# Taking two exponentials ahead of a single PSUM copy on ScalarE, in a software-pipelined attention kernel

## The chip, the core and the metric

One NeuronCore of a Trainium2 chip runs the whole program. The metric is device time in microseconds of one execution; for the kernel before, the median of 3 runs is 1517.59 us (1516.69 to 1521.7).

## What is computed

Eight images of 32x32 tokens with 192 channels go through two blocks, each with a normalisation ahead and a residual behind. The first is attention over the 1024 tokens with 12 heads of 16 channels; the second is a Fourier mixer with a per-token linear layer beside it. Cut to what matters:

```python
x = x + attention(group_norm(x), w_qkv, w_o)      # softmax(q k^T / 4) v, 12 heads, 1024 tokens
x = x + fourier_mixer(group_norm(x), w1, b1, w2, b2, bias_w, bias_b)
# mixer: rfft2 over 32x32, two complex 48x48 block layers with relu, irfft2, + x @ bias_w.T + bias_b
```

## The kernel before, in words

The work is a pipeline over images, written out by hand and fully unrolled: `body(b, prep, post)` for b = 0 to 7, between a prologue and a tail, once for each engine. A body has 48 **steps** (`u`, three groups of four heads by 16 key/half tiles). In each step:

- TensorE makes four **score tiles** of 128 keys by 512 queries (L1215) into three PSUM banks `scores`, and the **value product** of the step before into `o_acc` (L1268).
- ScalarE takes the exponential of each score tile into `probs` (L931). At steps with s = 9 and s = 0 it also copies the attention output out of `o_acc` (`take_o`, L939).
- TensorE makes four **max tiles** for attention 11 steps ahead, q times k again with the queries on partitions (L1247), and VectorE reduces each to its row maximum (L1023). Max 1 to 4 below are these four of one step.
- SP issues every DMA, in an order fixed by the program.

Beside this run the **pieces**: the preparation of image b+1 (`prep`: transposes `turn`, statistics, q/k and v products) and the rest of image b-1 (`post`: output projection, transposes, spread of the normalisation's factors, Fourier transforms `dftw`, `dfth`, mixing `mix1`, `mix2`, the inverses, and `lin`, the linear layer). TensorE makes a piece into PSUM; ScalarE copies it out for turn, spread, v, dftw, dfth, mix1, mix2 and idfth, VectorE for the others (q/k takes both). Tables `PREP_AT` and `POST_AT` say at which step a piece runs and in which of two places: at the **head** of the step (START) or in its **middle** (MID). The kinds of `PAIRED` (qk, v, proj, lin) enter as two entries, each with a PSUM bank of its own.

The order on TensorE within a step is: head pieces, max 1, score 1, max 2, score 2, value product of the step before, middle pieces, score 3, max 3, score 4, max 4. Max and score tiles use different halves of the array's rows, and are issued as neighbours. On ScalarE it is: take_o at s = 9, head pieces, exponentials 1 and 2, take_o at s = 0, middle pieces, exponentials 3 and 4. A score tile waits for the exponential three tiles back (`probs_made`, three banks).

Pieces and max tiles share the PSUM tile `ring`, of four banks. `RING_ORDER` lists everything that goes into it in TensorE's order, entry n uses bank n % 4, and `bank_free` makes TensorE wait, ahead of entry n, until the engine that reads entry n-4 is done with it:

```python
    for u in range(IN_BODY):
        out += pieces_at(u, START) + [("max", u, 0), ("max", u, 1)]
        out += pieces_at(u, MID) + [("max", u, 2), ("max", u, 3)]
        ...
```

`jobs_of` gives ScalarE's and VectorE's list of pieces of a step's head or middle, each with its bank. The list holds an entry also for a piece that the other engine takes; the piece function then returns without an instruction.

What reads the copies next: SP regroups rows by DMA behind each dftw copy (`regroup_rows`, L671), behind dfth (`stack_spectrum`, L680), mix2 (`regroup_mixed`) and idfth (`regroup_lines`). The same queue issues the stacks of q and k (L616, L621) and the shift rows (L630) that the first score tile of every eighth step waits for. VectorE's statistics read the transposes, POOL's `normalise_tokens` the spread.

Of the kernel before, what the change touches and what calls it, by code (L numbers as in the profile page):

```python
# [46 lines left out]
START, MID = 0, 1  # L47
# [87 lines left out]
def made(order, kind, k):  # L135

    return order[kind, k | 1 if kind in PAIRED else k] + 1
# [8 lines left out]
def on_act(kind):  # L146

    return kind in ON_ACT
# [109 lines left out]
def build(nc, consts, x, w_qkv, w_o, w1, b1, w2, b2, bias_w, bias_b, out):  # L258
# [3 lines left out]
    with ctx:  # L262
# [134 lines left out]
        def after(eng, s, count):  # L397

            if not isinstance(count, int) or count > 0:
                eng.wait_ge(s, count)  # L400
# [16 lines left out]
        def batches(eng, prologue, body, tail):  # L417

            prologue()
            body(0, True, False)  # L420
            for b in range(1, NB - 1):
                body(b, True, True)
            body(NB - 1, False, True)
            tail()

        def spectrum_piece(k, bank_):

            chunk, kk = divmod(k, 3)
            if kk == 2:
                return spec[:, chunk, :, 448:NF], bank_[0:CH, 0:C].rearrange("p (r f) -> p r f", r=2)  # L430
            n = 4 - kk
            src = bank_[0:CH, 0:P * n].rearrange("p (j r f) -> p r j f", j=n, r=2)
            return spec[:, chunk, :, 256 * kk:256 * kk + 64 * n].rearrange(
                "p r (j f) -> p r j f", j=n), src

        def hidden_piece(k, bank_):
            blk, half = divmod(k, 2)
            return (hidden[0:CH, blk, NF // 2 * half:NF // 2 * (half + 1)], bank_[0:CH, 0:NF // 2],
                    mix_a_bias[:, blk:blk + 1])
# [7 lines left out]
        def early_bank(no):  # L447
            return scores[:, no % EARLY_BANKS, :]

        def late_bank(kind, k):  # L450
            return late_banks[POST_NO[kind, k] % LATE_BANKS]

        def ring_bank(entry):
            return ring[:, RING_NO[entry] % RING, :]
# [26 lines left out]
        def pieces_of(b, u, part, prep, post):  # L481

            late = post and not (isinstance(b, int) and b < 2)
            return [e for e in pieces_at(u, part)
                    if (prep if e[0] == "prep" else late if e[1] == 2 else post)]

        def jobs_of(b, u, part, prep, post, prep_piece, post_piece):

            return [(prep_piece if e[0] == "prep" else post_piece, b - e[1], *e[2:], ring_bank(e))
                    for e in pieces_of(b, u, part, prep, post)]  # L490
# [6 lines left out]
        def late_pieces(post_piece):  # L497

            for n, (kind, k) in enumerate(in_order(LATE)):
                post_piece(NB - 2, kind, k, ring[:, n % RING, :])  # L500
# [22 lines left out]
        def token_tile(k):  # L523

            return k // 2 + NT // 2 * (k % 2)

        def token_quarter(k):

            at = HALF * (k % 2) + QUARTER * (k // 2 % 2)
            return slice(at, at + QUARTER)  # L530
# [392 lines left out]
        @block.scalar  # L923
        def _(act):
            def exponentials(b, g, s, h):
                n = g * TILES + s * GH + h
                act.wait_ge(scores_made, NG * TILES * b + n + 1)
                if h == 0:

                    after(act, pv_made, STEPS * NG * b + STEPS * g + s - 1)  # L930
                nc.scalar.activation(probs[:, GH * (s % 2) + h, :], scores[:, n % SCORE_BANKS, :], ACT.Exp,  # L931
                                     scale=SCALE).then_inc(probs_made, 1)

            def take_o(slot, half):
                act.wait_ge(pv_made, STEPS * slot + 8 * half + 8)
                if half == 0:

                    after(act, o_normed, slot)
                nc.scalar.copy(o_raw[:, HALF * half:HALF * (half + 1)],  # L939
                               o_acc[:, 0, :]).then_inc(o_out, 1)  # L940

            def prep_piece(b, kind, k, bank_):
                if kind != "qk" and not on_act(kind):
                    return
                act.wait_ge(prep_made, N_PREP * b + made(PREP_NO, kind, k))
                if kind == "turn":
                    nc.scalar.copy(xt[:, k, :], bank_).then_inc(prep_by_act, 1)
                if kind == "v":

                    after(act, v_ready, NG * b)  # L950
                    nc.scalar.copy(v_new[:, token_tile(k), :], bank_[:, 0:C]).then_inc(prep_by_act, 1)  # L951
                if kind == "qk":

                    for g in range(2 if k < 4 else NG):
                        after(act, stacked[g], STACK_INCS * b)
                        after(act, stacked_second[g], SECOND_INCS * b)
                    nc.scalar.copy(qk_parts[:, 0, k // 4, token_quarter(k)],  # L957
                                   bank_[:, 0:QUARTER]).then_inc(part0_done, 1)

            def post_piece(b, kind, k, bank_):  # L960
                if not on_act(kind):
                    return
                act.wait_ge(post_made, N_POST * b + made(POST_NO, kind, k))
                two = bank_[:, 0:2 * C].rearrange("p (t n) -> p t n", t=2)
                done = post_by_act
                if kind == "turn":
                    nc.scalar.copy(xt1[:, k, :], bank_).then_inc(done, 1)  # L967
                if kind == "spread":
                    nc.scalar.copy(affine[:, :, :], two).then_inc(done, 1)
                if kind in ("dftw", "idfth"):  # L970
                    nc.scalar.copy(rows_a[:, 2 * k:2 * k + 2, :], two).then_inc(done, 1)  # L971
                if kind == "mix2":
                    n = P if k < 4 else SIDE
                    nc.scalar.copy(mixed[0:n, k, :], bank_[0:n, 0:2 * C]).then_inc(done, 1)
                if kind == "dfth":
                    nc.scalar.copy(*spectrum_piece(k, bank_)).then_inc(done, 1)
                if kind == "mix1":
                    to, src, bias = hidden_piece(k, bank_)
                    nc.scalar.activation(to, src, ACT.Relu, bias=bias).then_inc(done, 1)  # L979

            def prologue():

                for no, (kind, k) in enumerate(PREP):
                    prep_piece(0, kind, k, early_bank(no))

            def body(b, prep, post):
                first = isinstance(b, int) and b == 0
                for u in range(IN_BODY):
                    g, s = divmod(u, STEPS)
                    slot = NG * b + g  # L990
                    if s == 9:
                        take_o(slot, 0)
                    for piece, *job in jobs_of(b, u, START, prep, post, prep_piece, post_piece):
                        piece(*job)
                    exponentials(b, g, s, 0)
                    exponentials(b, g, s, 1)
                    if s == 0 and not (first and g == 0):
                        take_o(slot - 1, 1)
                    for piece, *job in jobs_of(b, u, MID, prep, post, prep_piece, post_piece):
                        piece(*job)  # L1000
                    exponentials(b, g, s, 2)
                    exponentials(b, g, s, 3)

            def tail():
                take_o(NG * NB - 1, 1)
                late_pieces(post_piece)
                for kind, k in POST:
                    post_piece(NB - 1, kind, k, late_bank(kind, k))

            batches(act, prologue, body, tail)  # L1010


# [574 lines left out]
```

## Time and profile before

| | |
|---|---|
| median of 3 runs | 1517.59 us |
| the profiled execution | 1528.75 us |
| its span | 1527.0 us |
| granted TensorE clock, mean | 0.96 of full |
| TensorE, VectorE, ScalarE busy | 1445.3, 1158.3, 1009.0 us |
| 1536 exponentials | 829.0 us |
| 1536 maxima | 975.2 us |

The profiled execution is one run of the program and 11.16 us longer than the median. In the timelines, neighbouring instructions of one line and engine are merged into one row: its duration is from the first start to the last end, and x4 says how many there are. PEld is the loading of TensorE's weights, PE the matmul itself. A note in brackets is the idle time of that engine ahead of the row, and what ended it.

### The profile page before, as it was taken

What the parts mean: (1) busy time and instruction counts of PE and PEld (TensorE: products, weight loads), DVE (VectorE), ACT (ScalarE), POOL (GpSimd) and SP (SyncE); (2) the same over time, 40 slices, a digit from 0 to 9 for tenths busy, and PEclk for the clock granted to TensorE, in tenths of its full rate; (3) what the DMA queues carried; (4) which work ended last, traced back from release to release, by engine and by line L of the source; (5) the groups of instructions that cost most, each with busy time, mean ns of one, the idle gap of its engine ahead of it and who ended that gap; (6) DMA issues with size and microseconds to landing.
All of it is one profiled execution on the core that took longest, in us unless ns stands there. A gap on an engine that the chain in (4) does not pass through costs nothing.

```text
span 1527.0 us, 27399 instructions
## 1 busy us (share of the span) xinstructions
PE 1445.3 (95%) x9972; PEld 695.3 (46%) x9972; DVE 1158.3 (76%) x2153; ACT 1009.0 (66%) x2017; POOL 187.6 (12%) x277
## 2 busy tenths in 40 slices
PE   7699989999999999999999999999999999999787
PEld 4344333444545454444545444544544443434354
DVE  3695888888789878987789878997799878874131
ACT  1064777577767777677767777677767777668312
POOL 2000000140001300140011300040012100030000
PEclk7696999999999999999999999999999999999988
DMA  4430312213332414323422324333431333211313
GB/s 113 73 64 2 84 29 61 62 56 81 80 92 64 87 45 103 78 68 76 92 85 58 82 69 85 71 83 65 89 85 43 78 91 77 66 35 50 77 28 80
DMA packets 101126, 107.19 MB, mean 70 GB/s; under 512 B 25152, under 2 KB 77824, under 8 KB 100992
## 3 DMA queue, kind: packets, MB, share of 16 engines
q1 hardware_dynamic: 100992, 105.44, 30.1%
q8 instruction: 80, 1.31, 0.4%
q14 instruction: 54, 0.44, 0.1%
HBM read 27.51 MB, written 6.68 MB: 22 GB/s over the span
## 4 chain that ended last, share of the span: by engine, by line
PE 80%; DVE 6%; DMA 6%; SPq 2%; issue 2%; POOL 1%; ACT 1%; DVEq 0%; POOLq 0%; ACTq 0%
PE o_acc L1268 22%; PE ring L1247 15%; PE scores L1215 15%; PE ring L1291 10%; DVE row_max L1023 5%; DMA inv_all<-inv_rows 4%; PE ring L1280 3%; PE ring L1400 2%; PE ring L1393 2%; PE ring L1387 2%; SPq L663 2%; PE ring L1379 2%; PE scores L1291 1%; PE ring L1302 1%; PE ring L1406 1%
## 5 line engine op out<-in xcount | busy, mean ns | idle before, releaser
L1023 DVE TENSOR_REDUCE row_max<-ring 128x1 f32<-128x512 f32 x1536 | 975.2, 683 | 185.6 <-PE ring L1247 179.0
L931 ACT ACTIVATE probs<-scores 128x512 f32<-128x512 f32 x1536 | 829.0, 600 | 281.3 <-PE scores L1215 280.3
L1247 PE MATMUL ring<-k_stack,q_stack 48*128 48x512 f32 x1536 | 594.6, 469 | 26.7 <-DVE row_max L1023 24.3
L1215 PE MATMUL scores<-q_stack,k_stack 50*128 50x512 f32 x1536 | 598.7, 465 | 1.3 <-ACT probs L931 1.2
L1268 PE MATMUL o_acc<-probs,v_aug 128*18 128x512 f32 x3072 | 412.1, 609 | 2.4 <-ACT probs L931 1.2
L1215 PEld LDWEIGHTS scores<-q_stack,k_stack 50*128 50x128 f32 x1536 | 246.9, 188 | 319.6 <-ACT probs L931 294.9
L1247 PEld LDWEIGHTS ring<-k_stack,q_stack 48*128 48x128 f32 x1536 | 249.3, 191 | 145.4 <-DVE row_max L1023 97.3
L572 POOL TENSOR_TENSOR inv_all<-o_raw,inv_all 128x1024 f32<-128x1024 f32 x23 | 54.5, 2371 | 594.3 <-DMA inv_all<-inv_rows 594.3
L1268 PEld LDWEIGHTS o_acc<-probs,v_aug 128*18 128x18 f32 x3072 | 52.2, 96 | 124.5 <-issue 88.3
L1291 PE MATMUL ring<-xt,w_qk 64*128 64x256 f32 x504 | 62.3, 379 | 0.0
L1291 PE MATMUL ring<-wo,o_t 64*128 64x192 f32 x366 | 39.5, 346 | 16.1 <-DMA o_t<-inv_all 16.1
L1291 PEld LDWEIGHTS ring<-xt,w_qk 64*128 64x128 f32 x504 | 48.8, 186 | 9.1 <-DVE row_max L1023 3.9
L1095 DVE TENSOR_TENSOR x<-ring,x 128x192 f32<-128x192 f32 x60 | 18.8, 352 | 36.5 <-PE ring L1291 36.5
L1076 DVE TENSOR_TENSOR qk_parts<-ring,qk_parts 128x256 fp32r<-128x256 f32 x84 | 31.6, 417 | 18.9 <-ACT qk_parts L957 18.7
L1291 PEld LDWEIGHTS ring<-wo,o_t 64*128 64x128 f32 x366 | 34.2, 199 | 22.1 <-DMA o_t<-inv_all 10.5
L871 POOL COPY v_aug<-v_new 128x512 f32<-128x512 f32 x24 | 14.3, 620 | 241.8 <-ACT v_new L951 212.2
L957 ACT CAST qk_parts<-ring 128x256 fp32r<-128x256 f32 x84 | 27.2, 375 | 22.7 <-PE ring L1291 22.7
L826 POOL TENSOR_TENSOR calc<-mean_var,calc 128x3 f32<-128x3 f32 x16 | 3.1, 194 | 316.2 <-DVE calc L1098 232.4
L971 ACT COPY rows_a<-ring 128x384 f32<-128x384 f32 x59 | 28.5, 483 | 19.4 <-PE ring L1406 9.3
L967 ACT COPY xt<-ring 128x512 f32<-128x512 f32 x22 | 12.9, 586 | 37.8 <-PE ring L1280 37.8
L1400 PE MATMUL ring<-mix_b,spec_a 97*128 97x96 f32 (+1 forms) x304 | 37.2, 274 | 0.7 <-ACT spec_a L979 0.7
L1400 PEld LDWEIGHTS ring<-mix_b,spec_a 97*128 97x128 f32 (+1 forms) x304 | 33.2, 176 | 8.4 <-issue 7.3
(152 smaller groups left out, 1112.6 us busy)
## 6 DMA issues: line engine op xcount, KB each, us to landing
q_stack<-qk_parts SPq DMA_DIRECT2D x288, 64.0 KB, 2.2
k_stack<-qk_parts SPq DMA_DIRECT2D x144, 128.0 KB, 4.3
inv_all<-inv_rows SPq DMA_DIRECT2D x24, 512.0 KB
rows_b<-rows_a SPq DMA_DIRECT2D x128, 96.0 KB, 2.8
spec_b<-spec_a SPq DMA_DIRECT2D x64, 102.0 KB, 2.3
x_in<-in_x_dram SPq DMA_DIRECT2D x8, 768.0 KB, 5.0
x_res<-in_x_dram SPq DMA_DIRECT2D x8, 768.0 KB, 4.7
o_t<-inv_all SPq DMA_DIRECT2D x192, 32.0 KB, 1.9
```

Of the source, the lines that this page charges most:

```text
L572: ops.tensor_tensor(inv_all[:, :], o_raw[:, :], inv_all[:, :], ALU.mult).then_inc(o_normed, 1)
L663: sp.dma_start(o_t[to:to + HD, g, :], inv_all[32 * h:32 * h + HD, HALF * half:HALF * (half + 1)]).then_inc(o_packed, 16)
L931: nc.scalar.activation(probs[:, GH * (s % 2) + h, :], scores[:, n % SCORE_BANKS, :], ACT.Exp, scale=SCALE).then_inc(probs_made, 1)
L1023: nc.vector.tensor_reduce(row_max[:, which, m:m + 1], max_bank(g, unit, i), AX.X, ALU.max).then_inc(max_taken, 1)
L1076: nc.vector.tensor_tensor(qk_parts[:, 1, k // 4, cols], bank_[:, 0:QUARTER], qk_parts[:, 0, k // 4, cols].bitcast(F32), ALU.subtract).then ...
L1215: mm(scores[:, n % SCORE_BANKS, :], k_stack[rows, 2 * g + hp, P * kt:P * (kt + 1)], q_stack[rows, g, half, hp, :], start=True, stop=True). ...
L1247: mm(max_bank(g, unit, i), q_stack[rows, g, half, hp, P * qt:P * (qt + 1)], k_stack[rows, 2 * g + hp, HALF * which:HALF * (which + 1)], st ...
L1268: last = mm(o_acc[32 * h:32 * h + VW, 0, :], v_aug[:, g, kt, h, :], probs[:, GH * (s % 2) + h, :], start=(kt == 0), stop=(kt == NT - 1), s ...
L1280: last = mm(bank_[ROWS * half:ROWS * (half + 1), P * t:P * (t + 1)], src[:, t + NT // 2 * half, third::THIRDS], ident, start=True, stop=True)
L1291: out.append(mm(banks[half][:, 0:n], lhs, rhs, start=(c == 0), stop=(c == 2)))
L1379: last = mm(bank_[:, 0:2 * C], const("fw"), tok_n[:, 2 * k:2 * k + 2, :], start=True, stop=True)
L1400: last = mm(to[:, :, blk, :], hidden[:, blk, P * k:P * k + n], mix_b[:, blk, :], start=True, stop=True)
```

## The change

Where the head list of a step has at most one entry, ScalarE now runs the step's exponentials 1 and 2 first and the head's piece after them. Steps with two or more head entries keep their order, and so do all other engines. No instruction is added or removed.

```diff
-                    for piece, *job in jobs_of(b, u, START, prep, post, prep_piece, post_piece):
+                    heads = jobs_of(b, u, START, prep, post, prep_piece, post_piece)
+                    few = len(heads) <= 1
+                    for piece, *job in [] if few else heads:
                         piece(*job)
                     exponentials(b, g, s, 0)
                     exponentials(b, g, s, 1)
+                    for piece, *job in heads if few else []:
+                        piece(*job)
                     if s == 0 and not (first and g == 0):
                         take_o(slot - 1, 1)
                     for piece, *job in jobs_of(b, u, MID, prep, post, prep_piece, post_piece):
```

## Rows read from the trace of the kernel before

**Rows 1.** The page, part 1: busy time, share of the span, instructions.

```profile
PE 1445.3 (95%) x9972; PEld 695.3 (46%) x9972; DVE 1158.3 (76%) x2153; ACT 1009.0 (66%) x2017; POOL 187.6 (12%) x277
```

**Rows 2.** Windows, body 3: length, busy PE, PEld, DVE, ACT, POOL; clock, DMA, GB/s.

```profile
591.20:759.90 168.70, 168.02 (x1234) 81.00 (x1232) 142.52 (x268) 125.64 (x252) 24.25 (x32) 1.00 0.34 78
```

**Rows 3.** Timeline, step 15 of body 3: start us, us, engine, line, instruction.

```profile
642.17 0.50 PE L1215 MATMUL scores<-q_stack,k_stack 50*128 50x512 f32 x1
...
642.29 0.59 ACT L967 COPY xt<-ring 128x512 f32<-128x512 f32 x1 [0.22 <-PE ring L1280]
...
642.77 1.09 ACT L931 ACTIVATE probs<-scores 128x512 f32<-128x512 f32 x2
...
643.28 2.47 DVE L1023 TENSOR_REDUCE row_max<-ring 128x1 f32<-128x512 f32 x4
...
643.83 0.29 PEld L1247 LDWEIGHTS ring<-k_stack,q_stack 48*128 48x128 f32 x2
643.83 0.72 PE L1247 MATMUL ring<-k_stack,q_stack 48*128 48x512 f32 x2
...
644.36 1.08 ACT L931 ACTIVATE probs<-scores 128x512 f32<-128x512 f32 x2 [0.50 <-PE scores L1215]
...
644.49 1.13 PE L1280 MATMUL ring<-cst,x 128*64 128x128 f32 x16
```

**Rows 4.** Timeline, step 25 of body 3.

```profile
674.91 1.08 ACT L931 ACTIVATE probs<-scores 128x512 f32<-128x512 f32 x2 [0.59 <-PE scores L1215]
...
675.88 0.59 ACT L939 COPY o_raw<-o_acc 128x512 f32<-128x512 f32 x1
...
676.35 0.51 ACT L971 COPY rows_a<-ring 128x384 f32<-128x384 f32 x1
...
677.61 0.73 PE L1247 MATMUL ring<-k_stack,q_stack 48*128 48x512 f32 x2
```

**Rows 5.** Groups by form, ScalarE: xcount | busy us, mean ns of one | idle before.

```profile
L971 ACT COPY rows_a<-ring 128x384 f32<-128x384 f32 x59 | 28.5, 483 | 19.4 <-PE ring L1406 9.3 <-PE ring L1379 8.0 <-PE ring L1412 2.0
...
L967 ACT COPY xt<-ring 128x512 f32<-128x512 f32 x22 | 12.9, 586 | 37.8 <-PE ring L1280 37.8
```

**Rows 6.** Timeline, step 2 of body 3, behind the piece of step 1.

```profile
597.42 0.68 DVE L1023 TENSOR_REDUCE row_max<-ring 128x1 f32<-128x512 f32 x1
...
597.64 0.52 PE L1247 MATMUL ring<-k_stack,q_stack 48*128 48x512 f32 x1
...
598.15 0.18 PEld L1247 LDWEIGHTS ring<-k_stack,q_stack 48*128 48x128 f32 x1 [0.34 <-DVE row_max L1023]
598.15 0.49 PE L1247 MATMUL ring<-k_stack,q_stack 48*128 48x512 f32 x1
```

**Rows 7.** Timeline, TensorE weight loads of the second q/k pair, behind step 16.

```profile
649.17 0.55 PEld L1291 LDWEIGHTS ring<-xt,w_qk 64*128 64x128 f32 x6 [0.35 <-DVE row_max L1023]
```

**Rows 8.** Timeline, step 43 of body 3, weight load of its score 2.

```profile
742.03 0.18 PEld L1215 LDWEIGHTS scores<-q_stack,k_stack 50*128 50x128 f32 x1 [0.42 <-ACT probs L931]
```

**Rows 9.** Timeline, step 37 of body 3, weight loads of the v pair.

```profile
719.75 0.95 PEld L1291 LDWEIGHTS ring<-wv,xt 64*128 64x128 f32 x12 [0.85 <-DVE row_max L1023]
```

**Rows 10.** Timeline, SP and weight loads, bodies 3 and 1.

```profile
676.88 2.08 SPq L671 DMA_DIRECT2D rows_b<-rows_a  x2
...
688.55 2.52 SPq L671 DMA_DIRECT2D rows_b<-rows_a  x4
...
695.42 2.74 SPq L630 DMA_DIRECT2D q_stack<-shift  x4
...
694.25 0.46 PEld L1387 LDWEIGHTS ring<-cst,rows_b 128*96 128x96 f32 x4 [0.85 <-DVE row_max L1023]
...
700.41 0.19 PEld L1215 LDWEIGHTS scores<-q_stack,k_stack 50*128 50x128 f32 x1
...
270.78 1.31 SPq L630 DMA_DIRECT2D q_stack<-shift  x2
...
273.99 0.19 PEld L1215 LDWEIGHTS scores<-q_stack,k_stack 50*128 50x128 f32 x2 [0.23 <-DMA q_stack<-shift]
```

## The prediction

> **What bounds the kernel now.** I read the page first. TensorE is busy for 95% of the span, VectorE 76%, ScalarE 66% [rows 1]. Cut by image, body 3 gives TensorE 168.0 us of 168.7 at full clock, with VectorE at 142.5 and ScalarE at 125.6 [rows 2]. So a delay of TensorE is a delay of the kernel unless another chain covers it, and ScalarE has 43 us of idle time an image that costs nothing. Whether ScalarE does a copy before or after two exponentials matters only through what waits for it. That is read from single steps; I call a time z+0.57 when it lies 0.57 us behind the start of the step's first score matmul.
>
> The PSUM ring has four banks and is handed out in program order: head piece, max 1, max 2, max 3, max 4. The head piece and **max 4** of the same step therefore share a bank, and TensorE cannot start max 4 before ScalarE has copied the piece out. In step 15 of body 3 (z = 642.17) [rows 3] the copy runs from 642.29 to 642.88, the two exponentials from 642.77 to 643.86, and the weights of max 3 and max 4 load at 643.83 and 643.94 (two loads, together 0.29 us, of 0.18 each). Max 4 ends at 644.55, and the next piece starts at 644.49. The copy is over 1.06 us before its bank is wanted: today's slack.
>
> **What the change does, priced.** It removes and adds no instruction. It moves one ScalarE copy behind two exponentials in the steps whose head list has one entry: for a full image 0, 1, 4 (next image's transposes), 14, 15, 16 (transposes), 22, 25, 26, 28, 31, 34, 35, 37, 42, 46. The projections, "lin" and the q/k and v products enter as pairs, so their steps stay; steps 5, 7, 9 and 18 hold a single piece that VectorE takes, with nothing to move on ScalarE.
>
> *The new place of the copy.* Score 1 ends at z+0.50, and an exponential starts as little as 0.03 behind its score (third: 644.36, score over at 644.33); I take z+0.57, today's 642.77 being z+0.60. Back to back, ScalarE starts one operation every 0.48 to 0.49 us (1.08 for two, of 0.60 each), also from exponential to copy: 675.39, 675.88, 676.35 [rows 4]. So: exponentials at z+0.57 and z+1.06, copy at z+1.54. With the durations of [rows 5] it ends at z+2.13 (transposes, 0.59) or z+2.02 (the kinds of 0.48: 26, 28, 34, 35, 37, 42, 46). Step 31's copy is half as wide. The third exponential, at z+2.19, is not touched.
>
> *The price at max 4.* A released load starts 0.05 behind its releaser: maximum over at 598.10, load at 598.15; and its matmul ends 0.49 behind that [rows 6]. So max 4's weights load at z+2.18 instead of z+1.77, and it ends at z+2.68 instead of z+2.38: **+0.30 us**. The 0.48 copies: load z+2.07, end z+2.56, **+0.18**. Step 31, with its shorter copy, comes within hundredths of the present load: 0. Copies lying ahead of take_o in steps 0 and 16 push it and the third exponential by 0.2, which nothing waits for.
>
> *Which steps pass it on.*
> - 0, 4, 14, 15 go into a single piece and from there along TensorE. VectorE takes max 4, the last of four maxima in 2.47 us from 643.28 [rows 3], at 645.07 = z+2.90, and a max 4 ending at z+2.68 is still in time. Full: 4 x 0.30 = 1.20.
> - 1 goes into a "lin" pair. The following step's second matmuls wait for VectorE's maximum (load 598.15, 0.34 idle); that maximum follows from max 3, which is not delayed. The first pair starts at 597.94 instead of 597.64, the second would end at 598.70 (first's end 598.46 plus the 0.24 between ends in [rows 3]) against 598.64: **+0.06**. By the same cover 28, 35, 46 (0.18) cost 0.
> - 16 goes into two q/k pairs; the second waits 0.35 for VectorE [rows 7], which covers 0.30: 0.
> - 42: the next step's score 2 waits 0.42 for step 42's third exponential, which is not late [rows 8]: 0.18 is covered: 0.
> - 22: its second matmuls are late already, held by VectorE's maximum as in [rows 6], so max 4 is too; what is left of 0.18 is under 0.05: 0.
> - 25: take_o stands first; z = 675.89, exponentials 676.43 and 676.92, copy 677.41 to 677.91, load 677.96, end 678.45 against 678.34 [rows 4]: +0.10. It passes.
> - 26 and 34: followed by a q/k pair whose second matmuls run on TensorE's own pace, and by a single piece: 0.18 each.
> - 37 is different: its ring goes piece, max 1, max 2, v pair, so the bank is wanted in mid-step. The v weights load at 719.75 = z+1.65 [rows 9]; the copy would end at z+2.02, the load start at z+2.07: **+0.42**, and v copies, maxima and five mix1 pieces follow in line. Full.
>
> *The queues.* SP's DMAs for step 25 start 0.02 behind the dftw copy (676.88), and SP then issues almost without a break until 698.2 [rows 10]. The copy ends 1.05 later, so this train comes up to 1.05 later. Its last row transfer (the fourth of 2.52 us from 688.55, so issued at 690.4, with 2.5 to landing as below) is wanted by dfth, whose weights load at 694.25; the shift rows (the fourth of 2.74 us, issued at 697.5) are wanted by step 32's first score, whose weights load at 700.41. In body 1 that wait shows: last issue at about 271.45, the score held 0.23 until 273.99, so landing takes about 2.5. That leaves 1.3 and 0.4, plus the 0.28 by which TensorE is late itself, against at most 1.05. Between 0 and 0.37; SP's own pauses take some of it, and I take 0.15. The other moved copies meet an SP queue that is busy (26, 28, 46) or slack of over 0.4 (31, 42). POOL's use of the spread copy stands behind its own multiply of the attention output.
>
> **Sum.** An image in bodies 2 to 6: 1.20 + 0.06 + 0.10 + 0.36 + 0.42 + 0.15 = 2.29; five are 11.45. Body 1 has no late piece of an older image behind step 4, and the bare step after it is covered as behind 42: 1.99. Body 0 has only steps 0, 1, 4: 0.36. Body 7 has no q/k, v or transposes of a next image: 14, 15, 25, 34 = 0.88. Together 14.7 us. The profiled execution took 1528.75 (span 1527.0), 11 above the median of 1517.59; the added waits do not depend on that, so against its own time I expect 1543 profiled and 1532.3 as a median. A measurement of this kernel tells about 0.3% (4.6 us) from no change.
>
> **The load and a rule.** In [rows 3] max 4's load stands 0.11 behind max 3's, and in [rows 6] a held matmul starts with its load: load and matmul are held together, and the 0.11 of the load is paid. The Trainium skill (TensorE: Matmul & The Clock Gate, The mechanism) says that TensorE pulls weight loads ahead of matmuls in flight when they go to other rows. By that rule the weights would lie ready, and only the matmul would be late; by it the sum would be 8.8 in place of 14.7. The trace disagrees wherever a bank is the thing waited for: the load waits too.
>
> **Rivals.**
> - *Loads run ahead*, with only the matmul held: max 4 starts at z+2.18 against z+1.99, +0.19 for a transpose (four pass), +0.08 for the others (two pass), 25 nothing, 37 +0.31, SP 0.15: 1.38 an image in five bodies, less in the other three, 8.8 in all: 1526.4. For it: loads do lie ahead within a step. Against: [rows 6]. 0.13.
> - *Nothing is absorbed*: six transposes 1.80, 25 0.10, six others 1.08, 37 0.42, SP 0.25 = 3.65 an image, about 24.7 in all: 1542. For it: VectorE is close behind, and the covers are as narrow as 0.05. Against: the idle times in [rows 7, 8]. 0.12.
> - *Hidden*: the copies come in time because max 4 is not what TensorE waits for, or the loss is taken up by VectorE's queue two steps on. 1518, at most 1522. Against: TensorE has 0.7 us of idle time in an image [rows 2]. 0.07.
> - *Faster*: the first two exponentials no longer stand behind a copy: 0.03 each in most steps (z+0.57 for z+0.60) and up to 0.3 in 22 and 25, where copy or take_o stood ahead; at most 1 an image, some 5 in all: 1512.5. It decides if a score or a value product waits for them. Score 4 needs the first one at z+1.77, and it is over at z+1.20 today; the value product waits for the fourth. 0.05.
>
> My forecast has 0.63. The range 1523 to 1541 takes in the lower price and most of the unabsorbed case. Faster 0.05, same 0.07, slower 0.88.
>
> **What the profile after would show.** Max 4's load with an idle time ended by the ScalarE copy (xt, rows_a or spec_a), some 0.4 us in steps 0, 4, 14, 15, and those steps 0.30 longer; step 1 nearly unchanged, 42 unchanged; step 37 longer by 0.42; ScalarE's busy time the same. If steps 14 and 15 keep their length, the bank rule is read wrongly; if steps 28, 35, 42 grow by 0.18, the covers are.

## The result, and the profile after

The changed kernel takes **1545.8 us** (median of 4 runs, 1537.42 to 1550.97), the kernel before, on the same chip, 1519.64 (4 runs, 1516.69 to 1523.37): a ratio of 1.0166 [1.0112, 1.0219]. It is slower by 26 us; the forecast was slower by 14.7, 1532.3 us with a range of 1523 to 1541. Run again on another chip: 1544.06 us beside 1522.15, 1.0155 [1.0131, 1.0178]. The direction was right, the size too small, and the result lies outside the range.

The page of the changed kernel (busy us, share of the span, instructions) answers to [rows 1]:

```profile
span 1534.6 us, 27399 instructions
PE 1447.3 (94%) x9972; PEld 706.2 (46%) x9972; DVE 1162.4 (76%) x2153; ACT 1009.6 (66%) x2017; POOL 187.4 (12%) x277
```

Same instructions, same busy times. Lines from about 1000 on stand four higher than before: L1219 are the scores, L1251 the max tiles, L1284 the transposes, L1295 the other products, L1410 (before L1406) the first inverse Fourier stage, idfth; L1027 is the maximum. The windows of bodies 2, 3 and 4 (first score to first score; the columns of [rows 2]):

```profile
413.90:587.00 173.10, 170.06 (x1234) 83.61 (x1232) 143.22 (x268) 125.78 (x252) 24.24 (x32) 1.00 0.32 76
587.00:760.90 173.90, 171.42 (x1234) 84.13 (x1232) 143.06 (x268) 125.62 (x252) 24.22 (x32) 0.99 0.33 75
760.90:933.60 172.70, 170.22 (x1232) 83.67 (x1230) 143.17 (x268) 125.74 (x252) 24.22 (x32) 1.00 0.33 76
```

Body 3 took 168.70 before and grew by 5.2, of which 2.8 are no effect of the change: a longer wait for the attention output (1.84 us, before 0.43) and a stretch at half the clock behind it. The other two grew by 3.24 and 3.01.

**The hold.** The timeline of step 15 of body 3 in the changed kernel, whose z is 641.78 (start, duration, engine, line, instruction; in brackets the idle time and what ended it):

```profile
641.78 0.73 PE L1219 MATMUL scores<-q_stack,k_stack 50*128 50x512 f32 x2
...
642.35 1.08 ACT L931 ACTIVATE probs<-scores 128x512 f32<-128x512 f32 x2 [0.95 <-PE scores L1219]
...
643.32 0.59 ACT L967 COPY xt<-ring 128x512 f32<-128x512 f32 x1
...
643.96 0.18 PEld L1251 LDWEIGHTS ring<-k_stack,q_stack 48*128 48x128 f32 x1 [0.23 <-ACT xt L967]
643.96 0.50 PE L1251 MATMUL ring<-k_stack,q_stack 48*128 48x512 f32 x1
...
644.39 0.36 PEld L1284 LDWEIGHTS ring<-cst,x 128*64 128x64 f32 x6 [0.25 <-issue]
```

Against [rows 3]: the copy runs at z+1.54 to z+2.13, max 4's weights load 0.05 behind its end at z+2.18, and not 0.11 behind those of max 3; the matmul is over at z+2.68, and the next piece starts at z+2.61. The step is 0.29 us longer than before. What ended the idle time ahead of all 1536 max tiles (us, times):

```profile
  DVE row_max L1027: 112.6, 239
  issue: 26.9, 52
  ACT xt L947: 5.9, 22
  ACT xt L967: 4.9, 21
  ACT spec_a L979: 2.3, 6
```

In the kernel before this list has the spec_a line, the same to the tenth, and neither of the xt lines: the copies of 43 transposes now hold a max tile, for 0.25 us each. The idle times behind the shorter copies (0.13 in steps 26 and 34) stand in it under none of these names.

**Step by step.** I took the length of each step (first score to first score) in both traces. The growth is the same to 0.02 in bodies 2 to 6 where a step's lateness comes from the bank (but for step 25 of body 2, 0.19, and step 47 of body 6), and scattered where it comes from a DMA:

| steps | forecast, us | measured, bodies 2 to 6 |
|---|---|---|
| 0, 4, 14, 15 | 0.30 each | 0.29 each |
| 1 with 2 | +0.06 | +0.30 -0.24 |
| 16 | 0 | +0.08 |
| 22 | 0 | 0 |
| 25 | +0.10 | +0.12 |
| 26, 34 | 0.18 each | 0.18 and 0.17 |
| 28 with 29, 35 with 36, 46 with 47 | 0 | +0.19 -0.19 |
| 42 with 43 | 0 | +0.16 -0.16 |
| 37 | +0.42 | +0.48 |
| 31 with 32 (shift rows) | in the 0.15 for SP | +0.03, +0.04, +0.36, +0.24, +0.13 |
| 44 (idfth) | 0 | +1.24, 0, 0, 0, +0.49; body 7: +1.53 |

The bank part comes to 2.25 an image, 11.3 in five, 1.9 in body 1 (step 4's 0.30 comes back in step 5), 0.3 in body 0 and 1.15 in body 7: **14.6 us**, 13.8 forecast. Behind steps 31 and 44 come 0.8 and 3.3: **4.1 us**, 0.9 forecast. That makes 18.7.

**Where the 4.1 come from.** SP's timeline behind step 42 of body 7, six row transfers for idfth, first before, then after; their start is the end of ScalarE's copy at the head of step 42:

```profile
1409.94 1.35 SPq L689 DMA_DIRECT2D rows_b<-spec_b  x2
...
1413.31 0.62 SPq L692 DMA_DIRECT2D rows_b<-spec_b  x1
```

```profile
1416.85 1.35 SPq L689 DMA_DIRECT2D rows_b<-spec_b  x2
...
1420.23 0.62 SPq L692 DMA_DIRECT2D rows_b<-spec_b  x1
```

TensorE's timeline behind them, before and after:

```profile
1415.92 0.50 PE L1215 MATMUL scores<-q_stack,k_stack 50*128 50x512 f32 x2
1416.35 0.91 PE L1406 MATMUL ring<-rows_b,cst 128*128 128x384 f32 x2
```

```profile
1421.62 0.50 PE L1219 MATMUL scores<-q_stack,k_stack 50*128 50x512 f32 x2
1423.61 0.56 PE L1410 MATMUL ring<-rows_b,cst 128*128 128x384 f32 x1 [1.49 <-DMA rows_b<-spec_b]
```

Before, idfth starts 3.04 us behind the last issue (1416.35 against 1413.31). After, without its wait of 1.49, it would have started 1.89 behind it, so the train has lost 1.15 us against TensorE. The last transfer also landed 3.25 us behind its issue, in before 2.46. Before had 0.46 to spare: 1.15 + 0.79 - 0.46 = 1.48. Body 2 waits 1.20 (landing 4.08, before 2.73), body 6 waits 0.47 (3.35, before 2.49); in bodies 1 and 3 to 5 landing takes 2.46 to 2.88 and idfth doesn't wait.

*Why the last transfer lands late.* It is a small one, and in body 2 of the changed kernel the DMA view of its time in flight (570.42 to 574.50) shows, beside the data queue, a packet of the queue that the profile calls instruction:

```profile
q1 hardware_dynamic: 708, 0.60, 59.4%
q8 instruction: 1, 0.02, 1.3%
...
rows_b<-spec_b SPq DMA_DIRECT2D x1, 24.0 KB, 4.1
```

The 14 traces hold 112 of these trains. In 29 of them the last transfer takes over 2.6 us (2.64 to 4.08), and in every one of the 29 such a packet starts 1.24 to 1.93 behind its issue. In 81 of the other 83 none starts within the first 2.0 us, and these take 2.44 to 2.51; the last two have one at 1.76 and 1.90 and take 2.56 and 2.46. The packets come at the same places of the program, in bodies 2, 3, 6 and 7. Before, they start 1.93, 2.35 and 2.36 behind the issue in bodies 2, 3 and 6, and in body 7 after the landing; with the train later by 1.4 they start at 1.27, 1.66, 1.65 and 1.68. No run moved these packets by themselves, so that they cause the late landing is inferred from where they coincide. Without the late landings bodies 2 and 6 would not have waited, and body 7 only 0.7: some 2.5 of the 3.3 are owed to them.

**What of the difference is not the change.** The profiled execution of after took 1537.42 us, only 8.7 more than before's 1528.75. A good part of the gap to 18.7 is TensorE's clock: before's execution has a stretch at half the clock (granted 0.50, that is 1.2 GHz) in body 7 which after's has not. First before, then after at about the same time:

```profile
1329.60:1343.30 13.70, 13.70 (x55) 5.92 (x55) 8.53 (x16) 6.75 (x13) 5.47 (x9) 0.50 0.29 97
```

```profile
1330.00:1343.70 13.70, 12.99 (x83) 5.57 (x80) 11.69 (x24) 9.71 (x20) 2.32 (x10) 1.00 0.24 69
```

Steps 19 to 22 of that body took 5.0 us longer in before for it. Before was also slower in the prologue by 3.8 us (mean granted clock 0.72, after 0.81) and in body 0 by 4.2 (0.91, after 0.94). Bodies 1 to 6, at a mean of 1.00 in both, took 1016.1 in before and 1033.9 in after: 17.8 us for them alone, 15.7 of it in the table and most of the rest in body 3.

One execution of the kernel of experiment 3 took 1903 us, at a clock of 0.642, and is left out of every mean here. Over the 186 other executions of all kernels, each beside its mean granted clock, the time falls by 0.94 us for every 0.001 of clock within one kernel, and what is left over scatters by 1.9 us. I use that below: "at equal clock" is a difference of means taken to one clock, 0.970, with the half-width of its 95% interval in brackets. Its base is all 73 executions of before, on three chips, 1520.4 us. By chip they stand at 1519.7 (experiments 1 to 4), 1521.6 (5 to 8) and 1520.3 (9 to 12), so the chip alone can shift a figure by about 1. For the change it is **21.8 us** (1.3) and, again, 20.7 (2.5), in the middle 21.3; against before on its own chip alone the second is 19.4 (2.7). So of the 26 us, some 2.6 go with the clock: the ten executions of after had a mean of 0.967, those of before 0.970.

### The profile page after: what moved, and what is told of

Same layout as the page of the kernel before. It is cut to its first block, busy times and chain, and to the rows that moved or that the text cites. A ratio compares the mean times of both kernels' runs of the same rounds, so it can differ in the third digit from the quotient of the medians.

```text
span 1534.6 us, 27399 instructions
## 1 busy us (share of the span) xinstructions
PE 1447.3 (94%) x9972; PEld 706.2 (46%) x9972; DVE 1162.4 (76%) x2153; ACT 1009.6 (66%) x2017; POOL 187.4 (12%) x277
## 4 chain that ended last, share of the span: by engine, by line
PE 78%; DVE 7%; DMA 6%; SPq 3%; issue 2%; ACT 1%; POOL 1%; DVEq 0%; POOLq 0%; ACTq 0%
PE o_acc L1272 21%; PE scores L1219 16%; PE ring L1251 14%; PE ring L1295 9%; DVE row_max L1027 6%; DMA inv_all<-inv_rows 4%; PE ring L1284 3%; PE ring L1404 2%; PE ring L1391 2%; PE ring L1397 2%; SPq L663 2%; PE ring L1383 2%; PE scores L1295 1%; PE ring L1306 1%; PE ring L1410 1%
## 5 line engine op out<-in xcount | busy, mean ns | idle before, releaser
L1027 DVE TENSOR_REDUCE row_max<-ring 128x1 f32<-128x512 f32 x1536 | 976.0, 683 | 192.1 <-PE ring L1251 183.3
L1251 PE MATMUL ring<-k_stack,q_stack 48*128 48x512 f32 x1536 | 609.1, 471 | 25.9 <-DVE row_max L1027 22.8
L1219 PE MATMUL scores<-q_stack,k_stack 50*128 50x512 f32 x1536 | 590.5, 462 | 1.4 <-ACT probs L931 1.3
L1219 PEld LDWEIGHTS scores<-q_stack,k_stack 50*128 50x128 f32 x1536 | 244.2, 186 | 316.8 <-ACT probs L931 297.5
L1251 PEld LDWEIGHTS ring<-k_stack,q_stack 48*128 48x128 f32 x1536 | 252.9, 189 | 154.1 <-DVE row_max L1027 89.7
L1295 PE MATMUL ring<-xt,w_qk 64*128 64x256 f32 x504 | 63.4, 380 | 0.0
L1295 PE MATMUL ring<-wo,o_t 64*128 64x192 f32 x366 | 39.2, 344 | 16.7 <-DMA o_t<-inv_all 16.7
L1295 PEld LDWEIGHTS ring<-xt,w_qk 64*128 64x128 f32 x504 | 51.5, 186 | 3.7 <-DVE row_max L1027 1.6
L1080 DVE TENSOR_TENSOR qk_parts<-ring,qk_parts 128x256 fp32r<-128x256 f32 x84 | 31.9, 420 | 19.2 <-ACT qk_parts L957 18.9
L1295 PEld LDWEIGHTS ring<-wo,o_t 64*128 64x128 f32 x366 | 34.0, 197 | 22.4 <-DMA o_t<-inv_all 10.4
L971 ACT COPY rows_a<-ring 128x384 f32<-128x384 f32 x59 | 28.5, 483 | 20.5 <-PE ring L1410 12.5
L1295 PE MATMUL ring<-bias_t,xt 64*128 64x192 f32 x360 | 40.7, 336 | 0.0
```

The lines of the kernel that those rows point to most:

```text
L1027: nc.vector.tensor_reduce(row_max[:, which, m:m + 1], max_bank(g, unit, i), AX.X, ALU.max).then_inc(max_taken, 1)
L1080: nc.vector.tensor_tensor(qk_parts[:, 1, k // 4, cols], bank_[:, 0:QUARTER], qk_parts[:, 0, k // 4, cols].bitcast(F32), ALU.subtract).then ...
L1219: mm(scores[:, n % SCORE_BANKS, :], k_stack[rows, 2 * g + hp, P * kt:P * (kt + 1)], q_stack[rows, g, half, hp, :], start=True, stop=True). ...
L1251: mm(max_bank(g, unit, i), q_stack[rows, g, half, hp, P * qt:P * (qt + 1)], k_stack[rows, 2 * g + hp, HALF * which:HALF * (which + 1)], st ...
L1295: out.append(mm(banks[half][:, 0:n], lhs, rhs, start=(c == 0), stop=(c == 2)))
```

## The experiments

The theories. *Bank and queue*: the time is the bank held by the late copy (14.6), plus DMAs that start later (4). *Clock*: more idle time makes the clock fall, which costs the rest. *Covered chain*: before waits in bodies 1 to 5 for the rows of the attention output, o_t (the projections at step 10, 0.4 to 2.6 us in its trace); later steps ahead of it would be hidden there. Most experiments are one line: the set of steps in which the change acts. Each text of expectation was written before its run.

**1. The piece between the two exponentials.**

```diff
                     exponentials(b, g, s, 0)
-                    exponentials(b, g, s, 1)
                     for piece, *job in heads if few else []:
                         piece(*job)
+                    exponentials(b, g, s, 1)
```

> A single head piece is copied between exponentials 1 and 2 of its step, not behind both. Bank theory (the loss is max 4 and the v pair held for the piece's bank): the copy starts at z+1.06 and ends at z+1.65, so its bank is free at z+1.70, ahead of max 4's weight load at z+1.77; nothing is held, except some 0.05 us at step 37's v pair. Within 2 us of the kernel before, about 1518 us. Queue theory (the loss is in DMAs that start later behind the copies of steps 25 and 42): these copies are still 0.5 us later than before, so about half of the unexplained 10 us stays, 1523 us. Clock theory (any idle TensorE time costs extra by a lower granted clock): no idle time is added, so as before.

Measured: 1520.9 us beside 1519.65, 1.0019 [0.9996, 1.0042]; at equal clock +1.7 (1.2). The copy is over 0.5 earlier, before the bank is wanted. The list ahead of the max tiles:

```profile
  DVE row_max L1027: 124.4, 264
  issue: 27.0, 52
  ACT spec_a L979: 2.3, 6
  DVE tok_n L1106: 1.1, 6
  DVE qk_parts L1080: 0.3, 1
  DVE shift L1043: 0.2, 1
  ACT xt L947: 0.2, 1
```

The holds are gone, and with them about nine tenths of the cost. What is left shows in waits of 0.54 and 0.72 for idfth's rows, and in steps 31 with 32 longer by 0.23 and 0.10, 1.6 together: the queue part, at a lateness of 0.5. (The queue theory had expected half of 10 us.)

**2 to 4. The steps in three sets.** Covered: 1, 16, 22, 28, 31, 35, 46. Copies with DMAs behind them: 25, 42. Passing it on: 0, 4, 14, 15, 26, 34, 37. Together these are all 16. Edit (and the same with the other sets):

```diff
-                    few = len(heads) <= 1
+                    few = len(heads) <= 1 and u in (1, 16, 22, 28, 31, 35, 46)
```

> The change in steps 1, 16, 22, 28, 31, 35 and 46 alone, whose delay the next step was read to cover. Bank theory with covers: max 4 ends 0.18 to 0.30 us later in each of them, and the following step is shorter by as much; 0.08 an image is left behind step 16 and 0.05 behind step 1, together 1 us, 1519 us. Without covers: 0.30 x 2 + 0.18 x 3 = 1.14 us an image, 8 in all, 1526 us. Clock theory: the idle time of TensorE ahead of max 4 is there whether it is covered or not; if that idle time lowers the clock, this kernel is 4 us or more slower than before though its steps add nothing.

> The change in steps 25 and 42 alone, whose copies SP waits for. Bank theory: step 25 longer by 0.12 us in seven images, step 42 covered by step 43: 1 us. Queue theory: in addition TensorE waits for DMAs that start 1.05 and 1.45 us later, at the first idfth piece behind step 44 (up to 1.5 us in some images, 3 in all) and at the score of step 32 (0.1 to 0.35 us in four images): 4 to 5 us over the kernel before, 1522 to 1523 us. If the whole of the unexplained part sits here it is 10 us, 1529.

> The change in steps 0, 4, 14, 15, 26, 34 and 37 alone, whose delay was read to pass on. Bank theory: 4 x 0.29 + 0.18 + 0.18 + 0.48 = 2.0 us an image in five bodies, 1.7 in body 1, 0.3 in body 0, 0.9 in body 7: 13 us, 1531 us. Queue theory adds nothing here, no copy of a DMA train but that of step 26 is moved. Clock theory: the added idle time lowers the granted clock, and the whole of the missing 10 us comes on top: 1540 us. Chain theory: step 0's take_o stands behind the late copy, so the attention output of the last group reaches the projection at step 10 about 0.3 to 0.6 us later than TensorE itself is delayed, 0 to 0.3 us more in an image.

| set | time, before | ratio | at equal clock |
|---|---|---|---|
| covered | 1524.99, 1519.65 | 1.0030 [1.0011, 1.0050] | +3.2 (1.3) |
| 25, 42 | 1526.2, 1519.65 | 1.0032 [1.0016, 1.0049] | +5.9 (1.1) |
| passing | 1532.85, 1519.65 | 1.0079 [1.0059, 1.01] | +12.4 (1.1) |

The sums: 21.5 for the three, 21.3 for the whole. The effects add up within the scatter. Against before on their own chip the three are 3.9, 6.6 and 13.1, 23.6 together.

In the traces every step of a set behaves as in the whole change. *Covered*: 1 with 2 +0.05, 16 +0.08, the other pairs cancel, 0.13 an image; that is 0.8 in all, and the clock-corrected time says 2 to 3 more, for which I found no wait. By its median this set is 5.3 above before, at a mean clock of 0.968 against 0.970: that is what the clock theory had expected of it (4 or more), and between the two bank forecasts for it, 1519 and 1526 us, the time alone does not decide. The steps of the trace do: the covers hold. *25, 42*: 25 +0.12; behind 44 TensorE waits 1.06, 0.48 and 1.20; 31 with 32 grows by 0.24, 0.07, 0.20, 0.16 in four bodies, and step 30 by 0.33 and 0.10 in two: 4.7 of 5.9. *Passing*: 0.29 in 0, 4, 14, 15, 0.18 in 26, 0.17 in 34, 0.48 in 37, all bodies alike, steps 31 and 44 unchanged. It has most of the holds that lengthen a step, and a mean clock of 0.9698, that of before, and 1532.85 where the clock theory had expected 1540: against that theory.

**5. The change again,** as the anchor of another chip.

> The changed kernel once more, for its time and its granted clock over more executions. Bank theory and the queue's part together, as the parts run singly add up (+13, +4, +6 us): 1541 to 1543 us at the clock that the kernel before has, +22 us. If the added idle time of TensorE also lowers the clock (0.967 against 0.970 so far), the clock stays under that of the kernel before by 0.002 or more, and the difference is 25 us; by chance theory, the two clocks come out equal and the difference is 22.

The numbers stand above: 1.0155 [1.0131, 1.0178], 21.9 us. The mean clock was 0.9670 beside 0.9696, lower by more than the 0.002 that the clock theory had named, while the difference was that of the chance theory, 22 and not 25. This run does not decide between them.

**6 and 7. The steps in two sets, by what reads the copy.** No DMA reads the copy: 0, 1, 4, 14, 15, 16, 22, 34, 35, 37. Queue: 25, 26, 28, 31, 42, 46.

> The change in the ten steps whose copies no DMA reads: 0, 1, 4, 14, 15, 16, 22, 34, 35, 37. Bank theory: 4 x 0.29 + 0.05 + 0.08 + 0.18 + 0.48 = 1.95 us an image in five bodies, 1.7, 0.3 and 0.8 in the others, 12.5 us, 1532 us. If queue theory holds that is all that these steps cost, and the whole of the remaining 10 us is in the other six. If the extra is instead something that every moved copy brings, this one measures 16 us or more.

> The change in the six steps whose copies feed DMAs of SP: 25, 26, 28, 31, 42, 46. Bank theory: 0.12 + 0.18 us an image, 28, 31, 42 and 46 covered: 2.1 us, 1522 us. Queue theory: the DMAs of steps 25 to 31 and of step 42 start later, TensorE waits for them behind step 44 and at step 32: 8 to 10 us, 1528 to 1530 us.

Measured: 1541.09 us, 1.0125 [1.0112, 1.0138] for the first. That is 18.9 above before, where the bank theory had expected 12.5 and "something that every moved copy brings" 16 or more. Its four executions had a mean clock of 0.964, and at equal clock it is +14.6 (1.0), or 13.4 against before on its own chip: the reading for the bank rests on that correction and on the trace. The second took 1528.38, 1.0045 [1.0031, 1.0058], +8.1 (0.8), or 6.8 against its own chip, a little under the 8 to 10 expected. The bank accounts for 12.7 in the first set's trace. In the second it accounts for 1.9, since only 25 and 26 pass theirs on. Its trace shows 3.2 more at step 44 (1.23, 0.51, 1.49) and 0.9 at 31 with 32; 1 to 2 remain that I can't place. So steps with little bank cost do cost 7 to 8 us, and at least half of it stands at waits for DMAs. The two sets add up to 22.7, or to 20.2 against their own chip, where the whole change costs 19.4.

**8. Is the chain of the attention output a cover?** Before, with the reciprocals of the softmax sums taken a step earlier:

```diff
-INVERT_AT = 2
+INVERT_AT = 1
```

> The kernel before with one number changed: VectorE takes the reciprocal of the softmax sums in step 1 of a group, not in step 2. In the profile before, the projection's first piece at step 10 waits 0.4 to 2.6 us in five images for a DMA chain that begins with this reciprocal at z+10.1 (z of step 0), though its input has landed by about z+4.5. With the reciprocal at about z+6.9 the chain is 3.2 us earlier, and the wait, 6.5 us in all, is gone: 1513 us, and less spread between runs. If something else (the DRAM round trip beside other transfers, or VectorE being held in step 1) takes its place: 1518 to 1520 us.

A miss. 1522.19 us, 1.0009 [0.9992, 1.0025]. The reciprocal moves from z(step 0)+10.13 to z+6.81, and POOL's multiply of the attention output still starts at z+23.1 to z+24.5 in bodies 1 to 5. SP's timeline of before says why:

```profile
601.78 0.35 SPq L647 DMA_DIRECT2D inv_rows<-sums  x1
604.07 0.39 SPq L595 DMA_DIRECT2D x_in<-in_x_dram  x1
604.51 0.58 SPq L652 DMA_DIRECT2D inv_all<-inv_rows  x1
```

SP stands at the image's load x_in (in program order at step 3, `LOAD_AT`), which must wait until the next image's transposes have read the old one, in step 4; the broadcast inv_all waits behind it. With the earlier reciprocal inv_rows is issued 3.3 us earlier (z+7.24), while x_in and inv_all keep their places (z+12.85 and z+13.3). Bodies 6 and 7 have no such load, and in them the earlier reciprocal did bring the multiply forward, by 2.2 and 2.7 us.

**9 and 10. The load later,** in before and in after:

```diff
-LOAD_AT = 3
+LOAD_AT = 6
```

> The kernel before with the load of the image after next issued in step 6 in place of step 3. In the profile before, SP stands at this load until TensorE has made the transpose at the head of step 4 (issue at 604.07), and the 512 KB transfer that spreads the inverted sums is issued behind it at 604.51 and runs beside it; that transfer is what the projection at step 10 waits for in the end, and an earlier reciprocal moved none of it. With the load behind it the spread goes out about 1.2 us earlier and alone: if that is the bound, the wait (5 to 8 us over five images in the profiles so far) is gone or nearly so, 1514 us. If the DRAM round trip itself takes the 10 us, the transfers land no earlier and it stays at 1519.

> The changed kernel with the same load moved to step 6. If the DMA chain ahead of step 10 is what covers step 4's 0.29 us today (four images, 1.2 us), the change costs 1.2 us more against its own base than the changed kernel does against the kernel before: 23 us at equal clock, so about 1538 us. If the chain covers nothing, 21 to 22 us as now, 1536 us. If the spread's transfer is not shortened by the move, 1542 us.

**Before with the load at step 6 takes 1510.8 us** (1508.34 to 1513.05) beside 1519.93: 0.9935 [0.9916, 0.9954], faster than both kernels. SP's timeline now has

```profile
594.83 0.35 SPq L647 DMA_DIRECT2D inv_rows<-sums  x1
596.27 0.56 SPq L652 DMA_DIRECT2D inv_all<-inv_rows  x1
...
606.99 0.44 SPq L595 DMA_DIRECT2D x_in<-in_x_dram  x1
```

and POOL's multiply of body 3, before and then with the load at 6:

```profile
614.43 2.37 POOL L572 TENSOR_TENSOR inv_all<-o_raw,inv_all 128x1024 f32<-128x1024 f32 x1 [24.59 <-DMA inv_all<-inv_rows]
```

```profile
603.90 2.37 POOL L572 TENSOR_TENSOR inv_all<-o_raw,inv_all 128x1024 f32<-128x1024 f32 x1 [20.99 <-DMA inv_all<-inv_rows]
```

The waits of TensorE for the attention output, in all (us, times, longest), before and with the load at 6:

```profile
PE ring L1291 <- DMA o_t<-inv_all: 16.1, 6, 9.7
```

```profile
PE ring L1291 <- DMA o_t<-inv_all: 10.5, 2, 9.5
```

The longest stands in the tail, at the last image's projection, and stays. The gain at equal clock is 7.8 (1.0), of which these waits show 5.6.

After with the load at 6 takes 1530.26, 1.0078 [1.0052, 1.0105], at equal clock +13.5 (1.3), that is 21.3 (1.6) above before with the same load (19.5 by the medians; the two forecasts for it, 1536 and 1538, were made from a base 9 us higher). The change costs the same with the waits for the attention output as without them: they covered nothing that a measurement can tell. And this kernel has every hold of the change at the highest mean clock of all kernels here, 0.9724 (before with load 6: 0.9722), which goes against the clock theory once more.

**11 and 12. Step 42 alone, step 25 alone.** Edits: `few = len(heads) <= 1 and u == 42`, and the same with 25.

> The change in step 42 alone. The copy ends 1.45 us later and with it the six transfers that regroup the mixed spectrum; they were 1.9 us early for the first inverse piece in five images and 0.6 us in the last. Queue theory: waits of about 1.2, 0.5 and 1.5 us behind step 44 in three images, as the profile after has them, 3 us, 1523 us. Bank theory alone: step 43 covers step 42's 0.16 us, 0.

> The change in step 25 alone. Bank theory: 0.12 us in seven images, 0.8 us. Queue theory: the train of 22 transfers that follows starts 1.05 us later, and the first score of step 32 waits for the shift rows by 0.1 to 0.35 us in four images: 0.7 us more, 1.5 us in all, 1521 us. If the train costs more than its visible waits (transfers pushed into others), 3 us or more.

Step 42 alone: 1523.61, 1.0032 [1.0018, 1.0046], at equal clock +2.7 (1.0). TensorE's waits in its trace, in all:

```profile
PE ring L1410 <- DMA rows_b<-spec_b: 2.7, 3, 1.2
```

They are 1.1, 0.5 and 1.2, in bodies 2, 6 and 7, as in the whole change; steps 42 and 43 cancel. One copy, moved by 1.42 us, costs 2.7 us by its DMAs alone. Step 25 alone: 1522.64, 1.0012 [0.9997, 1.0027], +1.1 (1.1), not clear of no change; in its trace 0.12 in step 25, waits for the shift rows of 0.33, 0.22 and 0.88, and one of 0.58 for dfth's rows in body 3.

## Why the prediction was right in direction and wrong in size

- *The bank* was right, to hundredths: z+0.57, z+1.54, z+2.13, z+2.18 and z+2.68 all stand in the trace, and so do the 0.30 and the 0.18.
- *Load and matmul held together*: right. In the trace above the load starts at z+2.18, with its idle time ended by the copy (0.23 us of it, where some 0.4 had been named; the lateness is as forecast). The rule that TensorE pulls weight loads ahead of matmuls in flight (the Trainium skill, TensorE: Matmul & The Clock Gate, The mechanism) does not help a tile whose bank isn't free in this kernel: by it a transpose step would be 0.19 longer, and it is 0.29. The program's wait for the bank (`bank_free`) stands ahead of the tile's load as well as its matmul; no run here had it between the two.
- *Passed on or covered*: right for 0, 4, 14, 15, 25, 26, 28, 34, 35, 42, 46 and 1. Step 16 costs 0.08 in place of 0. The signs named beforehand were worded too simply: steps 28, 35 and 42 did grow, by 0.19, 0.19 and 0.16, and step 1 by 0.30, which was to mean that the covers are misread; but a cover acts in the step behind, and each of those is shorter by as much (0.24 behind step 1).
- *37* was mis-sized, 0.42 for 0.48. Read again, the v weights load at 720.75 with z = 718.63, z+2.12 and not z+2.07: [1.33 <-DVE row_max L1027], the idle time of TensorE's loads in the trace. I haven't found what the 0.05 is.
- **The failed step is "The queues"**, and in it the sentence "The other moved copies meet an SP queue that is busy (26, 28, 46) or slack of over 0.4 (31, 42)", with 0 for them. The copy of step 42 ends at z+0.57 before and at z+1.99 after, 1.42 later (the prediction has z+2.02); a slack of 0.4 could not cover that. I had asked if there was slack, and not how much against the shift. In the trace of before, idfth starts 1.9 us behind the landing of the last of the six in bodies 3 to 6, 1.06 and 1.63 in 1 and 2, and 0.59 in body 7; 0.13 to 0.14 of each is the least time from a landing to the start. Only body 7 was short of slack by itself, for 0.7 us. The rest came of landings of up to 4.08 us for the 2.5 that I had taken as fixed, in the places where the moved train coincides with instruction packets. With the shift rows (0.8, in the 0.15 an image that was asked) the queue costs 4.1 and not 0.9, a step off by 3.2.
- *From profile to median.* The forecast put all on the median of 1517.59. Beside the runs of after, before took 1519.64, 2 us more; and the executions of after had 0.003 less clock, 2.6 us. These are part of the 13.5 by which the forecast missed. That the lower clock is no effect of the change is argued from experiments 4 and 10, which have the holds without it; the whole change and experiment 6 did have low means (0.967, 0.967, 0.964), so it isn't shown.
- *What stays open.* At equal clock the change costs 21.3, and the waits that the traces show add up to 18.7. Against before on its own chip the repeat costs 19.4 (2.7), and then nothing is left over. The rest has the same sign in the covered set, in 6 and in 7, each about 2, of which the choice of base accounts for 1.3 in 6 and 7 and works the other way in the covered set. The waits for the attention output vary from execution to execution by that much, and their mean could have moved; no experiment here tells.
- *The rivals.* "Loads run ahead", "hidden" and "faster" are out by the timeline of step 15. "Nothing is absorbed" named 1542, nearer to the result than the forecast, and for the wrong reason: the covers hold, in every body.

Of the 26 us: 14.6 bank, 4.1 DMAs, 2.6 clock, this last an estimate from the fit; 4.9 are left, of which 2.6 is the open part and the rest lies within the interval of the ratio, 17 to 33 us for medians of four.

## What to carry to other kernels

Where tiles share a ring of banks, a copy's slack is the distance to the next tile in its bank, and it is read from one step to a few hundredths: behind one exponential this copy was free, behind two it cost 0.30 us a time. If a moved instruction releases DMAs, compare the shift with the slack of the last of them in every repetition of the step, since the last body had a third of the usual slack here, and do not take the landing time as fixed: a train that moves can meet traffic that it had passed by, here the instruction queue's packets. And look for what an in-order queue stands at: a load that waits for a buffer held up the broadcast behind it, and moving it by three steps was worth 0.65%.

## What I had not expected of the hardware

- The last of the six transfers for idfth, 24 KB, lands 2.46 us behind its issue in one body and 4.08 in another, and the late ones are those with an instruction packet beside them in flight. The 512 KB broadcast inv_all landed 9.9 us behind its issue (604.51 to POOL's start at 614.43) right behind the 768 KB load, and 7.6 us (596.27 to 603.90) issued by itself; over bodies 1 to 5 it is 9.8 to 11.0 and 7.6 to 8.8.
- The granted clock falls to half for stretches at places that differ between executions of one kernel. The 73 executions of before lie between 1512.4 and 1526.4 us, with mean clocks from 0.976 to 0.962. In the trace of after one stretch, which its repeat on another chip has not, begins right behind a wait of 1.84 us for the attention output: the engine's timeline, and the window behind it:

```profile
621.17 1.21 PE L1295 MATMUL ring<-wo,o_t 64*128 64x192 f32 x11 [1.84 <-DMA o_t<-inv_all]
```

```profile
622.30:625.70 3.40, 3.40 (x18) 0.97 (x16) 1.82 (x4) 1.09 (x2) 0.00 (x0) 0.50 0.67 192
```

  The waits of 1.20 and 1.49 us at step 44 have none right behind them: the granted clock is 1.00 from 574.60 to 580.00 and from 1423.60 to 1430.00.
